# A quantised stage re-ordered: the LoRA query from turned rows, the terms of x on ACT and GpSimd, the row scaling on ACT, batch 0's LoRA tiles among batch 1's tiles

## What is computed

```python
def fake_quant(x, s, z):
    q = jnp.clip(jnp.round(x / s + z), 0.0, 255.0)
    return (q - z) * s

def _L0_ffn_ref(x, W_org, lora_down, lora_up, lora_keys, Wq):
    base = jnp.einsum('bsi,oi->bso', x, W_org)
    q = jnp.einsum('bi,ki->bk', x.mean(axis=1), Wq)
    scores = jnp.einsum('bk,ek->be', q, lora_keys) / math.sqrt(K)
    coeffs = jax.nn.softmax(scores, axis=-1)
    h = jnp.einsum('bsi,eir->bser', x, lora_down)
    delta = jnp.einsum('be,bser,ero->bso', coeffs, h, lora_up)
    return base + delta

x = x + jnp.tanh(g_xattn[0]) * matmul(fake_quant(_layernorm(x), ...), fake_quant(ctx_4096, ...))
x = x + jnp.tanh(g_ffn[0]) * _L0_ffn_ref(_layernorm(x), ...)
x = x + jnp.tanh(g_xattn[1]) * _L1_xattn_ref(_layernorm(x), ctx_4096, ...)
x = x + jnp.tanh(g_ffn[1]) * _L1_ffn_ref(_layernorm(x), ...)
```

## Time and profile before

| what | us |
|---|---|
| median of 3 runs | 1386.14 |
| lowest, highest | 1383.67, 1386.9 |
| the profiled execution | 1389.39 |
| its span | 1387.6 |
| PE busy in it | 1289.6 (93%) |
| DVE busy | 840.5 (61%) |
| ACT busy | 446.8 (32%) |
| GpSimd busy | 648.2 (47%) |

### The profile page before, as it was taken

The page is one execution under the profiler, slowest core; times in us unless marked ns, Lnnn a source line. Parts: engine busy times, 40 slices in busy tenths (PEclk is TensorE's granted clock), DMA queues, the critical chain, the costliest instruction groups (busy, mean ns, idle before and its releaser), DMA issues.

```text
span 1387.6 us, 18180 instructions
## 1 busy us (share of the span) xinstructions
PE 1289.6 (93%) x6986; PEld 555.8 (40%) x6986; DVE 840.5 (61%) x1450; ACT 446.8 (32%) x804; POOL 648.2 (47%) x272
## 2 busy tenths in 40 slices
PE   5798778999998879999999999999979999999998
PEld 3455545444443322222222322224534444444443
DVE  7983991143344447888888888824466954363622
ACT  3683011101110026666666666671212101010000
POOL 5005615350003336778778877883014653453510
PEclk9989787999999989999999999999999999999999
DMA  8382213020004210010000001000023442452401
GB/s 311 115 304 72 80 47 91 31 61 0 0 25 138 75 58 18 19 36 18 19 27 27 18 18 35 1 1 1 0 81 122 140 144 91 148 164 67 137 0 60
DMA packets 38621, 97.17 MB, mean 70 GB/s; under 512 B 6160, under 2 KB 16400, under 8 KB 38544
## 3 DMA queue, kind: packets, MB, share of 16 engines
q1 hardware_dynamic: 37392, 91.94, 20.8%
q10 hardware_dynamic: 1152, 4.19, 0.7%
HBM read 85.49 MB, written 10.49 MB: 69 GB/s over the span
## 4 chain that ended last, share of the span: by engine, by line
PE 78%; DVE 15%; issue 2%; POOL 2%; ACT 2%; DMA 1%; SPq 0%; ACTq 0%; POOLq 0%; DVEq 0%
PE bank L559 46%; PE bank L767 12%; PE bank L754 8%; PE bank L806 6%; DVE mxp L1346 3%; PE bank L574 2%; PE bank L578 2%; PE bank L634 1%; DVE xn L1187 1%; DVE R L1152 1%; POOL R L535 1%; DVE XTl L1246 1%; DVE xn L1336 1%; DVE lnv L1184 1%; DVE R L1493 1%
## 5 line engine op out<-in xcount | busy, mean ns | idle before, releaser
L1346 DVE TENSOR_REDUCE mxp<-bank 128x1 f32<-128x512 f32 x512 | 317.4, 679 | 62.2 <-PE bank L754 61.5
L535 POOL TENSOR_TENSOR R<-R 128x2048 f32<-128x2048 f32 x64 | 290.2, 4535 | 80.2 <-ACT R L1073 80.2
L1073 ACT ACTIVATE R<-bank 128x512 f32<-128x512 f32 x512 | 271.7, 603 | 147.3 <-PE bank L806 145.2
L559 PE MATMUL bank<-XTh,R 128*128 128x512 bf16 x896 | 274.1, 383 | 10.0 <-POOL R L547 8.3
L480 POOL TENSOR_TENSOR R<-stage_w,zero 128x1024 f32 x36 | 70.1, 1946 | 358.2 <-DMA stage_w<-wts_in 230.2
L559 PE MATMUL bank<-R 128*128 128x512 bf16 x960 | 209.3, 379 | 2.3 <-DVE R L1528 2.0
L559 PE MATMUL bank<-XTl,R 128*128 128x512 bf16 x448 | 171.8, 383 | 0.0
L547 POOL TENSOR_TENSOR R<-stage_w,R 128x1024 bf16<-128x1024 f32 x32 | 76.1, 2392 | 172.2 <-DVE R L1493 172.2
L754 PE MATMUL bank<-R 96*128 96x512 bf16 x352 | 131.7, 385 | 15.0 <-DVE mxp L1346 11.0
L767 PE MATMUL bank<-R,stage_c 128*32 128x512 f32 x1024 | 137.5, 609 | 5.9 <-POOL stage_c L511 5.7
L559 PEld LDWEIGHTS bank<-R 128*128 128x128 bf16 (+1 forms) x960 | 93.8, 98 | 116.0 <-DVE R L1528 2.5
(11 more groups left out here) (174 smaller groups left out, 1467.0 us busy)
## 6 DMA issues: line engine op xcount, KB each, us to landing
stage_w<-wts_in SPq DMA_DIRECT2D x36, 512.0 KB, 3.6
stage_w<-w_in SPq DMA_DIRECT2D x32, 512.0 KB, 3.5
stage_c<-w_in SPq DMA_DIRECT2D x32, 512.0 KB, 3.5
R<-q_scr SPq DMA_DIRECT2D x48, 128.0 KB, 2.4
XTh<-ctx_nat_in SPq DMA_DIRECT2D x11, 512.0 KB, 4.7
XTh<-ctx_t_in SPq DMA_DIRECT2D x9, 512.0 KB, 5.2
X<-x_in SPq DMA_DIRECT2D x8, 512.0 KB, 7.1
q_scr<-R SPq DMA_DIRECT2D x32, 128.0 KB, 1.8
```

Source lines behind the costliest of these rows:

```text
L535: pool.tensor_tensor(PS[j % 2], PB[2 * j % 4], PB[2 * j % 4 + 1], ALU.add).then_inc(p_add, 1)
L559: mm = pe.matmul(o, a, m, start=first and a is ah and bs is bh, stop=last and a is al)
L1073: act.activation(PB[kt % 4][:, h * S:(h + 1) * S], bank[t_bank(g, t)][:, :], ACT.Exp, scale=float(HD) ** -0.5).then_inc(exp_done, 1)
L1346: dve.tensor_reduce(mxp[head // REP % 2][:, m, n // 2, n % 2:n % 2 + 1], bank[s_bank(u)][:, :], AX.X, ALU.max).then_inc(s_max, 1)
```

## The change

In the quantised stage and the LoRA stretch the work is spread and ordered anew. The sums are the same up to rounding.

- The addition of row and column term leaves DVE. ACT adds the row term to all of x during the context chunks (`add_rows`), GpSimd the column term (`add_columns`), four tiles ahead of the down weights' splits and four between them.
- ACT writes the normalised rows as x times scale plus bias (`scale_rows`); DVE only computes the bias. In the inverse root, which all norms share, two small operations with two tensor inputs become tensor_scalars with pointer operands.
- `turn_behind` comes two tiles behind the quantised matmul, and the one-column matmuls are gone. The LoRA query is a matmul of the query weights (now split by GpSimd, loaded early) with all 512 turned rows of a batch; DVE sums its columns (`lora_mean`).
- The query, shares and hidden tiles go batch by batch; batch 0's stand between the last tiles of batch 1. Quantised rows are turned into banks 6 and 7 between the first matmuls, and the second column sums come after two tiles.

```diff
+H_BANK = (7, 6, 7, 6, 1, 6, 7, 2)
+LQ_BANK = (6, 0)
...
-        LQW = R[5][:, 0:2 * KT * P].bitcast(F32)
+        LQW = stage_c[0]
+        lqw_h, lqw_l = (stage_c[1][:, :].bitcast(BF16)[:, i * KT * P:(i + 1) * KT * P] for i in range(2))
...
-            load_weights(WT_AT["down"], 4)
-            load_weights(WT_AT["org"], 2)
+            load_weights(WT_AT["down"], 2)
+            sp.wait_ge(c_done, len(CHUNKS))
+            sp.dma_start(LQW[:, :], lora_q).then_inc(lqw_in, 16)
             keys_out(1)
-            load_weights(WT_AT["org"] + 2, 4)
-            sp.wait_ge(nat_mm, TT)
-            sp.dma_start(LQW, lora_q).then_inc(lqw_in, 16)
-            load_weights(WT_AT["org"] + 6, 2)
+            load_weights(WT_AT["down"] + 2, 2)
+            load_weights(WT_AT["org"], 8)
...
+            def add_columns(b):
+
+                pool.wait_ge(cb_done, 2 * (b + 1))
+                for t in range(b * TB, (b + 1) * TB):
+                    pool.wait_ge(x_row, t + 1)
+                    xt = X[:, t * D:(t + 1) * D]
+                    pool.tensor_tensor(xt, xt, CB[:, b, :], ALU.add).then_inc(x_pre, 1)
+
+            def split_down(i):
+                split(WT_AT["down"] + i, i % 2, down_h[:, ds(i, D)], down_l[:, ds(i, D)])
+
+            add_columns(0)
+            split_down(0)
+            split_down(1)
+            add_columns(1)
+            pool.wait_ge(lqw_in, 16)
+            pool.tensor_tensor(lqw_h, LQW[:, :], zero[:, :].to_broadcast([P, KT * P]), ALU.add).then_inc(lqw_hi, 1)
+            pool.wait_ge(lqw_hi, 1)
+            pool.tensor_tensor(lqw_l, LQW[:, :], lqw_h, ALU.subtract).then_inc(lqw_done, 1)
+            split_down(2)
+            split_down(3)
...
             def turn_quantised(t):
-                if t >= 4:
-                    pe.wait_ge(xq_t, t - 3)
+                if t >= 2:
+                    pe.wait_ge(xq_t, t - 1)
                 for k in range(KT):
-                    mm = pe.transpose(bank_b[t % 4][:, k * P:(k + 1) * P], XQ[:, t * D + k * P:t * D + (k + 1) * P],
+                    mm = pe.transpose(bank_b[6 + t % 2][:, k * P:(k + 1) * P], XQ[:, t * D + k * P:t * D + (k + 1) * P],
                                       identb[:, :])
                 mm.then_inc(xq_turned, 1)
...
+            def lora_query(b):
+
+                pe.wait_ge(t_lo, 2 * TB * (b + 1))
+                for k in range(KT):
+                    r = slice(k * D + b * S, k * D + (b + 1) * S)
+                    w = slice(k * P, (k + 1) * P)
+                    mm = triple([bank[LQ_BANK[b]][:, :]], lqw_h[:, w], lqw_l[:, w], [XTh[:, r]], [XTl[:, r]],
+                                k == 0, k == KT - 1)
+                mm.then_inc(lq_mm, 1)
+
...
+            pe.wait_ge(c_done, CHUNKS.index(("N", 0, KT - 1)) + 1)
+            pe.wait_ge(v_dve, 4)
+            turn_quantised(0)
+            turn_quantised(1)
+            pe.wait_ge(v_act, 4)
+            column_sums(0)
+            turn_quantised(2)
+            pe.wait_ge(k_lo, 8)
+            quantised_tile(0)
+            turn_quantised(3)
+            turn_quantised(4)
+            quantised_tile(1)
+            turn_quantised(5)
+            turn_quantised(6)
+            pe.wait_ge(c_done, len(CHUNKS))
+            pe.wait_ge(cb_done, 2)
+            column_sums(1)
+            turn_quantised(7)
+            quantised_tile(2)
+            pe.wait_ge(cb_done, 4)
+            turn_behind(0, 0)
+            for t in range(3, TT - 1):
+                quantised_tile(t)
+                turn_behind(t - 2, t % 2)
+            pe.wait_ge(lqw_done, 1)
+            pe.wait_ge(xq_t, TT)
+            lora_query(0)
+            quantised_tile(TT - 1)
+            turn_behind(TT - 3, 1)
+            lora_scores(0)
             pe.wait_ge(wt_done, WT_AT["org"])
             lora_hidden(0)
-            pe.wait_ge(co_step, 1)
-            for b in range(B):
-                mm = pe.matmul(bank[5][0:1, b * E_LORA:(b + 1) * E_LORA], lq[:, b:b + 1], keys[:, :], start=True, stop=True)
-            mm.then_inc(sc_mm, 1)
+            lora_spread(0)
+            turn_behind(TT - 2, 0)
+            pe.wait_ge(cv_done, 2)
             lora_hidden(1)
-            pe.wait_ge(co_step, 6)
-            pe.matmul(bank[6][:, 0:B * E_LORA], onesf[0:1, :], coef[0:1, 3, :], start=True, stop=True).then_inc(bc_mm, 1)
-            for u in range(2, B * JT):
-                lora_hidden(u)
+            turn_behind(TT - 1, 1)
+            pe.wait_ge(h_lo, 1)
+            lora_hidden(2)
+            pe.wait_ge(h_lo, 2)
+            lora_hidden(3)
+            pe.wait_ge(x_up, 2 * TT)
+            lora_query(1)
+            lora_hidden(4)
+            lora_scores(1)
+            pe.wait_ge(h_lo, 4)
+            lora_hidden(5)
+            lora_spread(1)
+            lora_hidden(6)
+            lora_hidden(7)
 
...
+            def add_rows(t):
+                act.wait_ge(rterm_done, 1)
+                act.activation(X[:, t * D:(t + 1) * D], X[:, t * D:(t + 1) * D], ACT.Identity,
+                               bias=rterm[:, t:t + 1]).then_inc(x_row, 1)
...
+            for i, n in enumerate(range(CH0 + TT, len(CHUNKS))):
                 chunk(n)
-            act.wait_ge(rowq_done, TT)
+                if i % 2 == 1 and 3 <= i < 3 + 2 * TT:
+                    add_rows(i // 2 - 1)
             kv_out(1)
...
+
+                root(TT + t, t % 2)
+                act.wait_ge(ln_bias, t + 1)
+                if t >= 2:
+                    act.wait_ge(turned, t - 1)
+                act.activation(xn[t % 2][:, :], X[:, t * D:(t + 1) * D], ACT.Identity, bias=lnv[t % 2][:, 6:7],
...
+            for t in range(TT - 1):
+                quantised_out(t)
+            scale_rows(0)
+            quantised_out(TT - 1)
+            scale_rows(1)
+            for t in range(2, TT):
+                turned_out(t - 2)
+                scale_rows(t)
+            lora_exp(0)
+            turned_out(TT - 2)
+            hidden_out(0)
+            hidden_out(1)
+            turned_out(TT - 1)
+            hidden_out(2)
+            hidden_out(3)
+            lora_exp(1)
+            for u in range(JT, B * JT):
...
-                dve.scalar_tensor_tensor(out=v[:, 3:4], in0=v[:, 2:3], scalar=v[:, 2:3], in1=v[:, 0:1],
-                                         op0=ALU.mult, op1=ALU.mult).then_inc(ln_step, 1)
+                dve.tensor_scalar(v[:, 3:4], v[:, 2:3], v[:, 2:3], v[:, 0:1], ALU.mult, ALU.mult).then_inc(ln_step, 1)
                 dve.wait_ge(ln_step, 8 * n + 6)
                 dve.tensor_scalar(v[:, 4:5], v[:, 3:4], -0.5, 1.5, ALU.mult, ALU.add).then_inc(ln_step, 1)
                 dve.wait_ge(ln_step, 8 * n + 7)
-                dve.tensor_tensor(v[:, 5:6], v[:, 4:5], v[:, 2:3], ALU.mult).then_inc(ln_step, 1)
+                dve.tensor_scalar(v[:, 5:6], v[:, 4:5], v[:, 2:3], None, ALU.mult).then_inc(ln_step, 1)
                 dve.wait_ge(ln_step, 8 * n + 8)
+
...
-                xt = X[:, t * D:(t + 1) * D]
-                dve.scalar_tensor_tensor(out=xt, in0=xt, scalar=rterm[:, t:t + 1], in1=CB[:, t // TB, :],
-                                         op0=ALU.add, op1=ALU.add).then_inc(x_pre, 1)
...
+                if t >= 2:
+                    dve.wait_ge(xn_done, TT + t - 1)
                 statistics(TT + t, x_tile(t), t % 2)
-                if t > 0:
-                    lo_parts(t - 1, t - 1)
-
-                apply(TT + t, x_tile(t), t % 2, lambda t=t: dve.wait_ge(turned, t - 1) if t >= 2 else None)
-            lo_parts(TT - 1, TT - 1)
-
-
-            dve.wait_ge(turned, TT)
-            dve.tensor_scalar(mean[:, :, :].rearrange("p b k -> p (b k)"), bank[6][:, 0:B * KT], 1.0 / S, None,
-                              ALU.mult).then_inc(mean_step, 1)
-
-
...
+            dve.wait_ge(k_out, 32)
+            column_terms(0)
+            quantised_update(0)
+            quantised_update(1)
+            column_terms(1)
+            dve.wait_ge(xq_turned, TT)
+            for t in range(2, TT - 1):
+                quantised_update(t)
+            lora_mean(0)
+            quantised_update(TT - 1)
+            lora_shares(0)
+            lo_parts(TT - 2, TT - 2)
+            hidden_lo(0)
+            hidden_lo(1)
+            lo_parts(TT - 1, TT - 1)
+            hidden_lo(2)
+            hidden_lo(3)
+            lora_mean(1)
+            lora_shares(1)
```

179 lines of the change are left out of this document (89 added, 90 removed).

## The result

| | before | changed |
|---|---|---|
| median of 4 runs, us | 1386.52 | 1350.74 |
| lowest, highest | 1383.67, 1390.21 | 1347.12, 1350.84 |
| the profiled execution | 1389.39 | 1347.12 |
| its span | 1387.6 | 1345.3 |

The changed kernel takes 0.9734 of the time of the kernel before, with a 95% interval of 0.9706 to 0.9762: it is faster by 2.7%. The prediction was 1345 us, in a range of 1339 to 1362; the median lies 5.7 us above it and inside the range.

A forecast was written before the change was run, and what follows sets the result against it. From 116.5 to 266 us PE was taken to wait, with DVE busy 77.78 of the quantised stage's 93.00. Terms of -42.0, -2.3 (first stage) and +3 (clock) took 1389.39 to 1348.1, less 3.25 to 1345; range 1339 to 1362.

The forecast's parts named there:

- What bounds the stage: Quantised stage and LoRA stretch, 116.5 to 266 us: PE waits there would shrink, token phase at 224.0, 42.0 us less.
- allowance for the clock: One tile and one turn of PE at half clock cost 3.4 us, of which 3 were allowed.
- DVE's tile: Quantised stage: a tile costs DVE 5.3 us, in place of 7.15, with GpSimd busy or not.
- rival (b): Tiny DVE operations: pointer operands wait for GpSimd like a second tensor, a tile of 10.3, 1388 to 1391 us; chance 0.05.
- PE's waits: PE's new chain: waits of 0.9 us for column terms, 0.6 per DVE-paced tile and 2.5 before the spread.
- Additions put at 2.27 each: GpSimd: eight column term additions of 2.27 us among the weight splits, up weights split by 214, 10 us ahead.
- Additions put at 1.24 us: ACT: eight row term additions, 9.9 us between 72 and 116.5, put at 0 cost; eight normalisings of 1.24.
- (d): Keys and values of batch 1: chunks late by ACT's additions, 3 us, inside the range; no chance given.
- The first stage, 2.3 us: Tile 0 of the first stage: shorter root operations end its clip earlier, 2.3 us less, between 0 and 4.1.
- Rival (a): DVE-paced tiles: PE at half clock needs 8.1 us per tile, 1350 to 1362 us; chance 0.14.
- The step that failed: End of the sum: the profiled execution stood 3.25 us above the median, so 1348.1 becomes 1344.8.

The follow-up runs named there:

- root_old: The changed kernel with the two small operations of the inverse root in their old form, as before the change: 1365.77 us.
- before_again: The kernel before, unedited, run and profiled once more: median 1386.95 us, ratio 1.0005 to the kernel before.
- root_only: The kernel before with only the two small operations of the inverse root changed to tensor_scalars with pointers: 1382.16 us, ratio 0.9969.
- after_again: The changed kernel, unedited, run and profiled once more, its profile being the typical one: 1350.64 us, 0.9742 of the kernel before.
- terms_on_dve: The changed kernel with the addition of row and column term back on DVE, none on ACT or GpSimd: 1359.94 us.
- scale_again: Second run of the changed kernel with the normalising of the quantised stage back on DVE: 1356.85 us.

## Why the prediction was right, and where it was off

- **What bounds the stage.** Right: PE's waits in the old stage, with DVE setting the pace. The token phase was put at 224.0, less 2.3, plus 3: 224.7. It starts at 225.0 in the typical profile and at 221.5 in the other. From the end of the keys and values, where the forecast put 107.5 us, and 110.5 with the allowance for the clock, it is 110.7 and 107.6. The agreement to 0.3 us at the start is in part luck, as the points on the first stage and the clock show.
- **DVE's tile.** Predicted 5.3, measured 5.34. The pointer operations were put at 0.19 with the gap and take 0.21 to 0.28; rival (b) holds only for two tensor inputs, as root_old shows (8.1 us). The prediction was not quite right that no row showed pointers: the normalising reads its mean and scale so, and took 2.35 us with GpSimd busy, but over 1024 columns; on 128x1 the answer had to come from the run.
- **PE's waits.** 1.4 for V (1.47 measured), 0.9 for the column terms (1.33), 0.6 per tile (0.82), 2.5 in front of the spread (3.17 and 3.75). The last was mis-sized by one term: the 0.6 us for the shares on DVE took no account of a 1x8 step that lasts to the end of GpSimd's running split, here 0.67 and 1.25 us in place of 0.22. That leaves 0.2 us of other difference.
- **GpSimd.** Additions put at 2.27 each (2.32 measured), the end of the up weights at 214 (210.3, and 211.9 in the typical profile). (The prediction's 10 us for the eight additions on DVE is 9.2 by the figure that it quotes; nothing hangs on it.) The slack of 10 us is 11 and 13, shown by four and twelve extra operations.
- **ACT.** Additions put at 1.24 us take 1.13 to 1.17, normalisings take 1.24 as put; the keys and values of batch 1 have no new gap (PE 43.17 of 43.21), so the 3 us of (d) did not come.
- **The first stage, 2.3 us.** Right against the first profile of before, and luck. The first `x24` piece of the chain in the keys of batch 1 stands at 77.41 there and at 74.75 and 75.21 in the changed kernel; but it stands at 75.23 in before_again, at 75.34 in root_old, which has the old root, and at 75.81 in root_only, which has the new one. The operations shrank as forecast (0.27 and 0.21 us), but the clip of tile 0, at 28.40 in the first profile of before and at 24.14 and 24.29 in the changed kernel, came at 24.48 in before_again with the old operations. The long collision in the earlier trace rows was that execution's own, and no profile shows a gain at this place.
- **The clock, 3 us.** The allowance was right in size by luck (2.46 in the typical profile) and wrong in place: not in the DVE-paced tiles, where the clock was 1.00, but behind the wait for the shares. Rival (a) did not come.
- **The step that failed** is the one from the profiled execution to the median. It said that the profiled execution of before stood 3.25 us above the median and took that off the changed kernel's time too. But that execution was slower in the stage that the change replaces (266.0 against 257.2), which the changed kernel does not inherit, and its remainder was short (1121.6 against 1124.2 and 1124.9 in the second profiles), which it does. So the sum from it, 1348.1, lacks 2.6 us in the remainder and 0.3 in the stage, and the 3.25 should not have been taken off: 1351.0, which is after_again's own time. The forecast gain of 41.3 us was too large for the same reason; 35.8 were measured.

So the gain of 36 us is made of: the stage without its root change, 20.6 (root_old against before), and the root change in the new order, 15.0. Counted in the other order it is 4.2 for the root change and 31.4 for the rest. How the 20.6 divide among the order of the turns, the one-column matmuls and the query is not shown.

## What to carry to other kernels

On DVE, give small operations beside a busy GpSimd one SBUF tensor and pointers: the same products cost 0.21 and 0.27 us in place of 1.2 to 2.1, and it is worth most where the order keeps GpSimd busy all the time. Ask of each wait of PE not only how long it is but what the clock does behind it: in the execution that waited 0.6 us longer 2.5 us went in slow matmuls behind it, and an independent piece of work in the gap won both. Take two profiles of the kernel before, and where their stage under change differs, say so in the range; a profile's distance from the median may not be carried over to the changed kernel.

## What the runs showed of the hardware that I had not expected

- A DVE operation of eight elements on one partition (tensor_scalar, SBUF to SBUF) lasted to the end of GpSimd's running instruction: 0.22 us with GpSimd idle, 0.50 to 1.95 in ten of the profiles, each time within 0.03 us of the end of the split where the split can be seen by itself, while those of 128x1 with one or two pointers never took over 0.28 in the changed kernel's profile. Why the one waits and the others don't, no run here tells. So DVE and GpSimd do not meet only at semaphores.
- A collision of DVE and GpSimd can cost both: the same addition took 1.28 us free and 1.35 to 3.16 under splits, and the split beside it 1.89 or 2.87.
- The length of a PE wait does not by itself tell the clock behind it. In front of the spread of batch 0's shares, the turn behind a wait of 3.17 us (changed) ran at full speed (1.09), but behind 2.87 (terms_on_dve) it took 1.50, behind 3.32 (scale_again) 1.90 and behind 3.75 (after_again) 1.97. Other things differ between those executions too, and no run tells what decides.
